# Causal attention of sixteen narrow heads: bf16 parts in one stacked contraction, or fp32 in four strips of the array

## The chip, the cores and the metric

The kernel runs on one core of one Trainium2 chip. The metric is the device time of one execution in microseconds. Before the change the median of three runs is 3485.97 us (3484.61 to 3486.74). A difference of about 0.2% can be told from no change.

## The reference, cut to what matters

The whole kernel is a stack of eight layers on x of 4 batches x 1024 tokens x 128 features, in fp32. The change touches the fifth one alone, causal attention with 16 heads of 8 features each:

```python
def _L1_attn_a_ref(x, WQ, WK, WV, WO):
    mask = jnp.where(jnp.triu(jnp.ones((S, S), dtype=bool), k=1), -jnp.inf, 0.0)
    Q, K, V = (heads(WQ), heads(WK), heads(WV))        # 16 heads of 8 features
    score = jnp.einsum('bhqd,bhkd->bhqk', Q, K) / jnp.sqrt(8)
    score = score + mask
    score = score - jnp.max(score, axis=-1, keepdims=True)
    score = jnp.exp(score)
    score = score / jnp.sum(score, axis=-1, keepdims=True)
    out = jnp.einsum('bhqk,bhkd->bhqd', score, V)
    return out.transpose(0, 2, 1, 3).reshape(B, S, E) @ WO

x = x + _L1_attn_a_ref(_layernorm(x), WQ, WK, WV, WO)
```

## The kernel before, in words

`causal_attention` (line 1010) normalises x, transposes it into FT (L169), projects it (L1277 for Q and K, L1282 for V), and then works in 16 rounds. A round is one batch and one group of four heads. In each round the scores are computed twice. The first pass (L1305) has queries on the partitions and gives only the maximum of each query's row: VectorE reduces each unit out of PSUM (L1450). The maxima are turned (L1313), negated (L1456) and put as extra rows under the queries. The second pass (L1328) has keys on the partitions; its contraction contains that extra row, so the maximum is already subtracted, and ScalarE takes the exponential into the tile PT (L1417). The value product (L1341) then multiplies 128 keys at a time, with four heads side by side in column groups of 32, accumulating in banks 6 and 7. Column 8 of each head's values is all ones, which gives the row's sum.

**bf16 parts.** Q and K are cut into three bf16 parts (L1399, L1432, L1393, L1227), written to DRAM (L1163) and loaded back by `load_round` (L1083, 18 transfers a round) as 9 x 8 = 72 rows, so that one bf16 matmul with 128 rows gives the products of all parts. The maxima, too, are cut into three parts on GpSimd (L1235 to L1242) and sit in three rows from row 96, which L1261 clears. The causal mask is added to a diagonal block by an identity matmul of 128 columns in bf16 (L1308, L1330).

**Units and rings.** The first pass has 38 units a round, each up to one PSUM bank of 512 columns (30 of 512 and 8 of 384); the second pass likewise. First-pass units go through the ring of banks 0 to 2: a unit may start when VectorE has reduced the unit three before it (`s1_free`). Second-pass units go through banks 3 to 5 with ScalarE (`probs`). TensorE's queue is one order written at build time: `items` gives each second-pass unit and each value product a cost, and the first-pass steps of the following rounds are spread between them in proportion. Round r holds the second pass of round r and the first pass of round r+1 from its 19th unit on, and the first 18 units (`LEAD`) of round r+2. A round has 12 value pieces (`items`), with other work between any two of them, so TensorE goes over to the values and back twelve times.

**The sums.** `invert` on SyncE's queue takes the row of sums to 128 partitions, VectorE inverts it (L1464), it goes to DRAM and back broadcast over 8 rows a head (L1193). `divide` multiplies on VectorE (L1468), and two steps a round (`out`, L1318) project the four heads with WO and add to x (L1460).

Of the kernel before, what the change touches and what calls it, by code (L numbers as in the profile page):

```python
# [7 lines left out]
F32 = mybir.dt.float32  # L8
# [6 lines left out]
P = 128  # L15
# [5 lines left out]
BANK = 512  # L21
# [988 lines left out]
def causal_attention(k):  # L1010

    nc, w, bank = k.nc, k.w, k.bank
    HEADS, HD, STRIP = 16, 8, 32
    GROUPS, IN, PARTS = 4, 4, 3
    ROUNDS, SLOTS, RING, SPACES = BATCH * GROUPS, 4, 3, 3  # L1020
    ROWS = PARTS * PARTS * HD
    PEAK = 96
# [3 lines left out]

    QK = k.big[:, 0:SLOTS * GROUP].bitcast(BF16).rearrange("p (s m t) -> p s m t", s=SLOTS, m=2)
    PT = k.big[:, SLOTS * GROUP:(SLOTS + 2) * GROUP].rearrange("p (s h t) -> p s h t", s=2, h=IN)
    FT = k.big[:, SLOTS * GROUP:(SLOTS + 1) * GROUP]
    REST = k.big[:, (SLOTS + 1) * GROUP:(SLOTS + 1) * GROUP + 2 * BANK].rearrange("p (s t) -> p s t", s=2)  # L1030

    parts = [k.big[:, at:at + PARTS * SEQ].bitcast(BF16).rearrange("p (m a t) -> p m a t", m=2, a=PARTS)
             for at in ((SLOTS + 1) * GROUP + 2 * BANK, (SLOTS - 1) * GROUP, (SLOTS - 2) * GROUP)]
# [3 lines left out]
    OT, INV, ON = (z.rearrange("p j d -> p (j d)") for z in zt[1:])  # L1037

    cleared = k.count("causal_cleared")

    def clear(sp, s):

        return sp.dma_start(QK[ROWS:P, s, :, :], k.dram["c_pads"])

    def clear_first(sp):
        for s in range(SLOTS - 2):
            clear(sp, s).then_inc(cleared.sem, 16)

    layernorm(k, turn=(FT, SEQ, 0), sp_first=clear_first)
    inverses = nc.dram_tensor("causal_inverses", (IN, SEQ), F32).ap()  # L1050
    kept = nc.dram_tensor("causal_parts", (2, BATCH, P, PARTS, SEQ), BF16).ap()

    names = ("qk_up", "first", "second", "left", "third", "v_up", "v_in", "fed", "s1_up", "s1_free", "s2_up", "probs",
             "pv", "vs_in", "o_in", "sums_out", "inverse", "sums_in", "peak", "split", "zeroed", "inv_kept", "divided", "ready")
    (qk_up, first, second, left, third, v_up, v_in, fed, s1_up, s1_free, s2_up, probs, pv, vs_in, o_in, sums_out,
     inverse, sums_in, peak, split, zeroed, inv_kept, divided, ready) = [k.count("causal_" + n) for n in names]
    written = [[k.count(f"causal_written{m}{b}") for b in range(BATCH)] for m in range(2)]
    loaded = [k.count(f"causal_loaded{s}") for s in range(SLOTS)]
    peaks_in = [k.count(f"causal_peaks_in{s}") for s in range(SLOTS)]
    with ExitStack() as mem:  # L1060
# [3 lines left out]
        mask = sb("mask", [P, 2, P], BF16)  # L1064
        REST6 = k.arena6[:, TOK:]
        WP = REST6[:, 0:2 * P].rearrange("p (m t) -> p m t", m=2)
        WS = REST6[:, 2 * P:6 * P].rearrange("p (g d) -> p g d", g=GROUPS)
# [3 lines left out]
        low = sb("low", [IN * TPB, 2, P])  # L1071
        lowb = sb("low_parts", [IN * TPB, PARTS, P], BF16)

        def load_round(sp, r, s):

            for m in range(2):
                of_round = kept[m].rearrange("b (g e h) a t -> (b g) e h a t", g=GROUPS, h=IN)
                of_round = of_round[r:r + 1] if isinstance(r, int) else of_round[bass.ds(r, 1)]
                of_round = of_round.rearrange("r e h a t -> (r e) h a t")
                for a in range(PARTS):  # L1080
                    for c in range(PARTS):
                        rows = slice((a * PARTS + c) * HD, (a * PARTS + c + 1) * HD)
                        sp.dma_start(QK[rows, s, m, :].rearrange("e (h t) -> e h t", h=IN), of_round[:, :, a if m else c, :]).then_inc(loaded[s].sem, 16)  # L1083

# [1969 lines left out]
```

## Time and profile before

| what | us |
|---|---|
| median of three runs | 3485.97 |
| the profiled execution, its own time | 3486.21 |
| span of its trace | 3484.3 |
| TensorE matmul busy | 2833.4 (81%) |
| VectorE busy | 2478.2 (71%) |
| ScalarE busy | 1756.8 (50%) |
| GpSimd busy | 1837.0 (53%) |

A busy share of the whole span is an average over eight layers with different limits; the layer that is changed has to be cut out by its window, from about 717 to 1368.7 us. The end of a matmul in the trace is modelled: a 512-column bf16 record is shown some 0.17 us longer than the array streams it, so records that follow each other overlap. In what follows the distance from start to start is used. An fp32 matmul shows as two records.

### The profile page before, as it was taken

The numbers are of one execution on the slowest core, as the hardware profiler recorded it, in microseconds if no ns is written. First come the engines' busy times: TensorE is split into PE (matmuls) and PEld (weight loads), VectorE is DVE, ScalarE is ACT, GpSimd is POOL, SyncE is SP. The second block draws the span as 40 slices with busy tenths as digits, with TensorE's granted clock in tenths as the row PEclk, the third lists the DMA queues.
The fourth block names the chain that finished last, engine by engine and source line by source line (L and its number), as shares of the span: only waits on it lengthen the run. The fifth ranks groups of instructions, "written<-read, shape, count | busy, mean of one in ns | idle before, by whom it ended". The sixth has DMA issues, their size and how long they took to land. (4 is left out here: it accounts for less than half of the span.)

```text
span 3484.3 us, 62796 instructions
## 1 busy us (share of the span) xinstructions
PE 2833.4 (81%) x22143; PEld 1662.3 (48%) x22143; DVE 2478.2 (71%) x4050; ACT 1756.8 (50%) x3569; POOL 1837.0 (53%) x1184
## 2 busy tenths in 40 slices
PE   3677468568999995999999993677677599999998
PEld 1211257443444442677667752223222277757774
DVE  5599646558777763777577755698599777767774
ACT  3544125134556553677467732544444277737762
POOL 3499211130111101888188822698299598729871
PEclk9699678779999997999999996899899899999999
DMA  3355000042222210112112210343054112211121
GB/s 90 79 162 151 8 7 1 8 116 69 38 44 38 44 24 24 38 40 47 30 36 44 43 25 5 109 158 121 31 169 157 56 40 44 45 24 42 42 45 40
DMA packets 176158, 203.21 MB, mean 58 GB/s; under 512 B 108358, under 2 KB 122396, under 8 KB 175388
## 3 DMA queue, kind: packets, MB, share of 16 engines
q1 hardware_dynamic: 175868, 199.41, 22.2%
q8 instruction: 174, 2.85, 0.4%
q14 instruction: 116, 0.95, 0.1%
HBM read 138.36 MB, written 9.44 MB: 42 GB/s over the span
## 5 line engine op out<-in xcount | busy, mean ns | idle before, releaser
L319 POOL TENSOR_TENSOR arena<-arena 128x1024 f32<-128x1024 f32 x192 | 451.3, 2351 | 61.1 <-DVE arena L336 34.0
L1450 DVE TENSOR_REDUCE causal_peak_parts<-psum 128x1 f32<-128x512 f32 (+3 forms) x608 | 375.9, 658 | 114.9 <-PE psum L1308 69.6
L2047 POOL TENSOR_TENSOR arena<-arena,w_minus_half 128x16 f32<-128x16 f32 x128 | 372.5, 2910 | 97.0 <-DVE arena L1954 97.0
L1417 ACT ACTIVATE arena<-psum 128x512 f32<-128x512 f32 (+1 forms) x608 | 304.0, 597 | 229.5 <-PE psum L1330 106.7
L1889 ACT ACTIVATE arena<-psum,arena 128x128 f32<-128x128 f32 x1024 | 277.8, 382 | 252.8 <-DVE arena L1963 252.8
L336 DVE TENSOR_TENSOR_SCAN arena<-psum,arena 128x1024 f32<-128x1024 f32 x160 | 364.6, 2280 | 27.9 <-POOL arena L319 27.9
L289 ACT ACTIVATE psum<-arena,w_A 128x1024 f32<-128x1024 f32 x192 | 214.5, 1118 | 248.5 <-DVE arena L336 211.4
L2054 POOL TENSOR_TENSOR arena<-arena 128x1024 f32<-128x1024 f32 x124 | 292.4, 2358 | 12.6 <-DVE arena L1948 12.6
L1734 PE MATMUL psum<-w_layer_wqkv,arena 128*128 128x512 f32 x512 | 262.7, 638 | 5.7 <-DVE arena L1948 3.7
L262 PE MATMUL psum<-arena,m_sel 96*128 96x512 bf16 x384 | 117.4, 388 | 180.6 <-DVE arena L351 153.0
L1959 DVE COPY arena<-psum 128x512 f32<-128x512 f32 x128 | 88.5, 691 | 238.0 <-PE psum L1746 238.0
L2059 POOL TENSOR_TENSOR arena<-arena 128x1024 f32<-128x1024 f32 x124 | 236.0, 1903 | 19.1 <-POOL arena L2050 19.1
L277 PE MATMUL psum<-arena,w_ident 128*128 128x512 f32 x512 | 243.4, 598 | 0.0
L1328 PE MATMUL psum<-arena 128*128 128x512 bf16 (+3 forms) x768 | 218.6, 331 | 23.5 <-ACT arena L1417 17.1
L1305 PE MATMUL psum<-arena 128*128 128x512 bf16 (+3 forms) x768 | 214.6, 330 | 21.1 <-DMA arena<-causal_parts 11.6
L262 PEld LDWEIGHTS psum<-arena,m_sel 96*128 (+1 forms) x384 | 23.5, 97 | 342.4 <-issue 174.5
L1954 DVE TENSOR_REDUCE arena<-arena 128x16 f32<-128x1024 f32 x128 | 155.1, 1212 | 31.2 <-ACT arena L1867 31.2
L2187 PE MATMUL psum<-arena,w_layer_w 128*128 128x512 f32 (+1 forms) x384 | 176.4, 595 | 0.0
L1341 PE MATMUL psum<-arena,Z 128*32 128x512 f32 (+3 forms) x1536 | 164.9, 503 | 0.3 <-ACT arena L1417 0.3
L179 POOL TENSOR_TENSOR ln_rstd<-ln_var,w_minus_half 128x8 f32<-128x8 f32 x32 | 53.1, 1659 | 208.9 <-DVE ln_var L108 208.9
L1963 DVE TENSOR_REDUCE arena<-psum 128x8 f32<-128x1024 f32 x128 | 156.6, 1224 | 9.2 <-PE psum L1771 9.0
L1328 PEld LDWEIGHTS psum<-arena 128*128 128x128 bf16 x768 | 72.2, 97 | 180.8 <-issue 81.3
(331 smaller groups left out, 6620.7 us busy)
## 6 DMA issues: line engine op xcount, KB each, us to landing
arena<-scan_rows_large SPq DMA_DIRECT2D x128, 512.0 KB, 3.7
arena<-arena SPq DMA_DIRECT2D x256, 130.0 KB, 2.6
arena<-scan_rows_small SPq DMA_DIRECT2D x128, 256.0 KB, 3.8
arena<-causal_parts SPq DMA_DIRECT2D x288, 64.0 KB
causal_parts<-arena SPq DMA_DIRECT2D x8, 768.0 KB, 9.0
arena<-Z SPq DMA_DIRECT2D x128, 32.0 KB, 1.9
arena<-Z SPq DMA_DIRECT2D x32, 128.0 KB
arena<-in_c_pads SPq DMA_DIRECT2D x4, 896.0 KB
```

Of the source, the lines that this page charges most:

```text
L277: mm = pe.matmul(bank[6 + c][0:M, :], fold, weight[:, s % 2, c * BANK:(c + 1) * BANK], start=False, stop=isinstance(j, int) and j == J - 1 ...
L319: pool.tensor_tensor(inputs[:, s % 2], b_lane[:, s % U], du(*runs[o]), ALU.mult).then_inc(input_up.sem, 1)
L336: dve.tensor_tensor_scan(state[s % U], decay(s), inputs[:, s % 2], 0.0, ALU.mult, ALU.add).then_inc(scanned.sem, 1)
L1305: mm = pe.matmul(o, QK[:, s, 0, col + qt * P:col + (qt + 1) * P], QK[:, s, 1, col + half * BANK:col + half * BANK + size], start=True, sto ...
L1328: mm = pe.matmul(o, QK[:, s, 1, col + kt * P:col + (kt + 1) * P], QK[:, s, 0, col + lo:col + hi], start=True, stop=True)
L1417: act.activation(PT[:, kt % 2, heads[0]:heads[0] + len(heads), lo:hi], place, ACT.Exp, scale=SCALE).then_inc(probs.sem, 1)
L1450: dve.tensor_reduce(part[:, heads[0]:heads[0] + len(heads), qt, half:half + 1].rearrange("p h a -> p (h a)"), place[:, 0:len(heads) * size ...
L1734: mm = pe.matmul(bank[pair_of(i) + m], HT[:, s4, :], w["wqkv"][:, m * INNER:(m + 1) * INNER], start=True, stop=True)
L1889: e = act.activation(PR[:, s, h, :], two(3)[:, h * P:(h + 1) * P], ACT.Exp, bias=LOW[:, s, h:h + 1])
L2047: pool.tensor_tensor(RN[:, s4, :], SS[:, s4, :], k.minus_half[:, 0:2 * HEADS], ALU.pow).then_inc(rn_in.sem, 1)
L2054: pool.tensor_tensor(COS[s4], COS[s4], SIN[s4], ALU.add).then_inc(ready2.sem, 1)
L2059: pool.tensor_tensor(heads, heads, RN[:, s4, :].unsqueeze(2).broadcast_to([P, 2 * HEADS, HD]), ALU.mult).then_inc(rot.sem, 1)
```

## The change

Nothing outside `causal_attention` and its constants changes.

- **Scores in fp32.** The parts, their DRAM tensor and the extra casts are gone. Q and K of all heads lie in QD as they come from the projection (ScalarE copies, `qk_in`). `load_round` issues 8 transfers, SBUF to SBUF, that put head i of a group at partitions 32i to 32i+7; row 32i+8 holds the maxima (queries) and ones (keys). A score matmul contracts 8 rows (first pass) or 9 (second pass) of one head's strip of 32 partitions.
- **One head per bank.** A unit is one head's tiles in one bank, 40 units a pass: in the first pass 28 of 512 columns, 8 of 384 and 4 of 256, heads in the order 0, 1, 2, 3; in the second 24 of 512 and 16 of 384, heads 2, 3, 0, 1.
- **Masks.** In the first pass a unit with diagonal blocks (24 of the 40) gets four bf16 matmuls of 32 rows, PICK x MASK, of together 320 columns per diagonal block. In the second pass there is none: GpSimd sets the probabilities of later keys to zero with `affine_select` in PT, 24 instructions a round (`cap_probs`), and the value product waits for them (`capped`).
- **Values.** The same matmuls, in seven visits a round instead of twelve (`follow`), both halves together.
- **Maxima.** No parts: one fp32 row per head is written by four transfers. `split_maxima` and the clearing of rows are gone from GpSimd.
- **Divide** moves from VectorE to GpSimd, between its selects, and waits for `packed`.
- **Output per batch.** `pack` (SyncE's queue) copies each group's 4 x 8 rows into OP; the projection with WO runs twice a batch instead of twice a round.
- **Beginning.** Four of the sixteen Q/K projections and all V projections come first, then scoring starts; the other twelve projections stand between the first pass's units of round 0, one after each second unit. `LEAD` is 20.

```diff
-                        sp.dma_start(QK[rows, s, m, :].rearrange("e (h t) -> e h t", h=IN), of_round[:, :, a if m else c, :]).then_inc(loaded[s].sem, 16)
+                heads = QD[STRIP * g:STRIP * (g + 1), m, b * SEQ:(b + 1) * SEQ]
+                for i in range(IN):
+                    sp.dma_start(QK[STRIP * i:STRIP * i + HD, s, m, :], heads[HD * i:HD * (i + 1)]).then_inc(loaded[s].sem, 16)
...
+        first_groups = [([(0, 0, [0]), (4, 1, [4])], (0, 2)), ([(1, 0, [0, 1]), (5, 1, [5, 4])], (1, 2)),
+                        ([(2, 0, [0, 1, 2])], (2, 1)), ([(3, 0, [0, 1, 2, 3])], (3, 1)),
+                        ([(4, 0, [0, 1, 2, 3])], None), ([(5, 0, [0, 1, 2, 3])], None), ([(6, 0, [0, 1, 2, 3])], None),
+                        ([(6, 1, [4, 5, 6])], (2, 1)), ([(7, 0, [0, 1, 2, 3])], None), ([(7, 1, [4, 5, 6, 7])], (3, 1))]
+        first_units = [(hh,) + u for u in first_groups for hh in range(IN)]
...
+        second_units = [(hh,) + u for u in second_groups for hh in (2, 3, 0, 1)]
...
+        follow = {10: [0], 18: [1], 26: [2], 30: [3], 35: [4], 39: [5], 3: [6, 7]}
...
+                def cap_probs(r, i):
+                    hh, tiles, slot, at, diag, done = second_units[i]
+                    pool.wait_ge(probs.sem, probs.at(r * N2 + i + 1))
+                    place = PT[:, slot, hh, at:at + diag * P].rearrange("p (d t) -> p d t", t=P)
+                    pattern = [[0, diag], [1, P]] if diag > 1 else [[1, P]]
+                    pool.affine_select(place, place, pattern, ALU.is_ge, 0.0, base=0, channel_multiplier=-1).then_inc(capped.sem, 1)
...
+                for r in range(ROUNDS):
+                    for n, i in enumerate(diagonal):
+                        if n == IN:
+                            values(r)
+                        if n == 4 * IN and r:
+                            divide(r - 1)
+                        cap_probs(r, i)
+                divide(ROUNDS - 1)
...
+                        for qt, half, keys in tiles:
+                            runs = [keys] if keys == sorted(keys) else [[x] for x in keys]
+                            for run in runs:
+                                size = len(run) * P
+                                mm = pe.matmul(out[:, at:at + size], QK[rows, s, 0, qt * P:(qt + 1) * P], QK[rows, s, 1, run[0] * P:run[0] * P + size],
+                                               start=at == 0, stop=True, skip_group_check=True)
...
+                            for c in range(4):
+                                mm = pe.matmul(place[:, :, STRIP * c:P], PICK[strip, c, :], MASK[strip, c, 0:diag[1], STRIP * c:P],
+                                               start=False, stop=True, skip_group_check=True)
...
+                for n, step in enumerate(scoring + [("turn", 0)]):
+                    ring_step(step, n, -1)
+                    if n % 2 and ahead < len(CH):
+                        project(ahead)
+                        ahead += 1
```

## Rows read from the trace of the kernel before

**Rows 1.** Busy time by window: us, then PE, PEld, DVE, ACT, POOL, clock, DMA.
```profile
717.00:734.00 17.00, 7.84 (x32) 6.09 (x32) 14.98 (x88) 9.44 (x22) 6.57 (x5) 0.54 0.50 108
734.00:769.50 35.50, 22.81 (x96) 14.39 (x96) 15.75 (x24) 17.93 (x32) 21.56 (x23) 0.82 0.43 115
769.50:805.50 36.00, 26.65 (x140) 10.39 (x140) 33.49 (x60) 1.28 (x1) 1.79 (x5) 0.94 0.62 191
1010.59:1045.28 34.69, 33.31 (x275) 15.12 (x274) 26.55 (x45) 19.81 (x40) 5.29 (x6) 1.00 0.23 43
1322.00:1352.00 30.00, 25.74 (x196) 9.59 (x194) 2.96 (x4) 20.50 (x40) 0.40 (x1) 0.92 0.03 6
```

**Rows 2.** ScalarE's copies of the output, one a round, rounds 1 to 15.
```profile
L1408 ACT COPY Z<-psum x15: 1007/1047/1047, 839.1 to 1324.1; 128x1024 f32<-128x1024 f32 x15
```

**Rows 3.** Timeline of TensorE: scores, then one value product of four heads, scores.
```profile
1000.92 0.22 PE L1308 MATMUL psum<-causal_mask,w_identb 128*128 128x128 bf16 x1
1001.07 1.06 PE L1341 MATMUL psum<-arena,Z 128*32 128x512 f32 x8
1002.07 0.39 PE L1328 MATMUL psum<-arena 128*128 128x512 bf16 x1
1002.29 0.22 PE L1330 MATMUL psum<-causal_mask,w_identb 128*128 128x128 bf16 x1
```

**Rows 4.** Timeline of ScalarE just behind: start, duration, releaser.
```profile
1002.55 0.60 ACT L1417 ACTIVATE arena<-psum 128x512 f32<-128x512 f32 x1 [2.73 <-PE psum L1330]
```

**Rows 5.** Timeline of TensorE: projections, a 2-matmul group and a 4-matmul group in turn.
```profile
739.64 1.88 PE L1277 MATMUL psum<-arena 128*128 128x512 f32 x4
741.36 1.05 PE L1282 MATMUL psum<-w_WV,arena 128*128 128x128 f32 x8
742.25 1.88 PE L1277 MATMUL psum<-arena 128*128 128x512 f32 x4
```

**Rows 6.** Another layer's fp32 scores in four 64x64 tiles: ns min/median/max, first and last start.
```profile
L1771 PE MATMUL psum<-arena x32: 268/269/270, 1500.7 to 1501.5; 64*64 64x128 f32 x32
```

**Rows 7.** Timelines of VectorE and ScalarE where several follow without a wait.
```profile
789.46 3.07 DVE L1450 TENSOR_REDUCE causal_peak_parts<-psum 128x1 f32<-128x512 f32 x5
1324.96 3.28 ACT L1417 ACTIVATE arena<-psum 128x512 f32<-128x512 f32 x7
```

**Rows 8.** Groups by line and form, 734 to 1368 us, VectorE: busy, mean ns, idle.
```profile
L1450 DVE TENSOR_REDUCE causal_peak_parts<-psum 128x1 f32<-128x512 f32 x384 | 249.1, 686 | 65.7 <-PE psum L1305 39.5 <-PE psum L1308 23.1
L1468 DVE TENSOR_TENSOR Z<-Z 128x1024 f32<-128x1024 f32 x16 | 19.5, 1219 | 9.9 <-DMA Z<-causal_inverses 9.9
```

**Rows 9.** The same for GpSimd; the last row is of a later layer (page).
```profile
L1261 POOL MEMSET arena<- 3x4096 bf16 x12 | 42.1, 3506 | 1.7
L1249 POOL COPY Z<-arena 128x256 f32<-128x256 f32 x16 | 6.3, 397 | 218.7 <-PE psum L1341 218.6 <-issue 0.2
L1216 POOL COPY arena<-w_WK 128x128 f32<-128x128 f32 x1 | 0.4, 402 | 0.0
L1227 POOL TENSOR_TENSOR arena<-arena 128x512 bf16<-128x512 f32 x16 | 18.4, 1158 | 6.2 <-ACT arena L1393 6.1
L2054 POOL TENSOR_TENSOR arena<-arena 128x1024 f32<-128x1024 f32 x124 | 292.4, 2358 | 12.6 <-DVE arena L1948 12.6
```

**Rows 10.** The beginning: SyncE's queue and the first score.
```profile
735.16 1.36 SPq L1155 DMA_DIRECT2D arena<-in_L_attn_a_WO  x4
751.17 13.07 SPq L1083 DMA_DIRECT2D arena<-causal_parts  x18
769.65 0.27 PE L1305 MATMUL psum<-arena 128*128 128x128 bf16 x1 [11.58 <-DMA arena<-causal_parts]
```

**Rows 11.** The end of the layer, in order of time.
```profile
1350.83 1.01 ACT L1408 COPY Z<-psum 128x1024 f32<-128x1024 f32 x1 [0.55 <-PE psum L1341]
1357.29 1.28 SPq L1193 DMA_DIRECT2D Z<-causal_inverses  x4
1360.76 1.23 DVE L1468 TENSOR_TENSOR Z<-Z 128x1024 f32<-128x1024 f32 x1 [4.94 <-DMA Z<-causal_inverses]
1362.04 3.78 PE L1318 MATMUL psum<-arena,Z 128*128 128x128 f32 x16 [11.28 <-DVE Z L1468]
```

More of the change, by code:

```diff
@@ L1300, in ring_step @@
                         out = enter(n)
-                        for at, hh in enumerate(heads):
-                            col = hh * SEQ
-                            o = out[:, at * size:(at + 1) * size]
-                            diag = half == (qt * P) // BANK
-                            mm = pe.matmul(o, QK[:, s, 0, col + qt * P:col + (qt + 1) * P], QK[:, s, 1, col + half * BANK:col + half * BANK + size],
-                                           start=True, stop=True)
-                            if diag:
-                                mm = pe.matmul(o[:, size - P:size], k.identb, mask[:, 0, :], start=False, stop=True, skip_group_check=True)
+                        at = 0
@@ L1362, in body @@
-                def body(r, s, before, more, b, g):
-                    steps = ring_steps(before, more)
-                    start = ring_start(r) if before else SHORT + LEAD
-                    fill = b + 1 + (1 if s == 0 and before else 0)
-                    pe.wait_ge(peaks_in[s].sem, peaks_in[s].at(fill * 16 * PARTS))
+                    for half in range(kt // 4, 2):
+                        lo = max(kt * P, half * BANK) - half * BANK
+                        for hh in range(IN):
+                            mm = pe.matmul(bank[6 + half][STRIP * hh:STRIP * (hh + 1), lo:BANK], VS[:, kt, hh, :], probs_place(kt, half, hh),
+                                           start=kt == 0, stop=kt == 4 * half + 3)
@@ L1367, in body @@
+                feed(1)
+                for n, step in enumerate(soon):
+                    ring_step(step, SHORT + n, -1)
+                pe.wait_ge(qk_in.sem, qk_in.at(len(CH)))
+                pe.wait_ge(v_in.sem, v_in.at(TOK // BANK))
+                for r in range(ROUNDS):
+                    steps, start = steps_of(r), ring_start(r)
+                    pe.wait_ge(peaks_in[r % SLOTS].sem, peaks_in[r % SLOTS].at(16 * IN * (r // SLOTS + 1)))
                     done, spent = 0, 0
-                    for kind, at, half, cost in items:
+                    for kind, at, cost in items:
@@ L1402, in _ @@
-                part_two(len(CH) - 1)
+                    act.copy(QD[:, m, c * BANK:(c + 1) * BANK], bank[i if i < 4 else 3 + i % 3]).then_inc(qk_in.sem, 1)
                 def outputs(r):
                     act.wait_ge(pv.sem, pv.at(TPB * (r + 1)))
-                    if not isinstance(r, int) or r:
+                    if r:
                         act.wait_ge(divided.sem, divided.at(r))
                     act.copy(OT, k.psum[:, 6 * BANK:8 * BANK]).then_inc(o_in.sem, 1)
-                def body(r, s, before, more, b, g):
-                    for i, (kt, heads, lo, hi) in enumerate(second_units):
-                        n, size = r * N2 + i, hi - lo
+                for r in range(ROUNDS):
+                    for i, (hh, tiles, slot, at, diag, done) in enumerate(second_units):
+                        n, size = r * N2 + i, sum(hi - lo for _, lo, hi in tiles)
```

458 lines of the change are left out of this document (188 added, 270 removed).

## The prediction, made before the changed kernel was run

> **What bounds the layer now.** I read the windows first: a full round [rows 1] has TensorE busy 33.3 of 34.7 us at full clock (the fourth row), VectorE 26.6, ScalarE 19.8, GpSimd 5.3. The copies of the output confirm the round: 14 steps in 485.0 us, 34.6 each [rows 2]. Busy TensorE is modelled, so I count columns. In bf16, 18432 columns of scores and 4096 of masks in each pass, at 2.4 columns per ns, are 18.8 us a round. An fp32 column costs 1.70 ns: two matmuls of 512 and four of 128 repeat after 2.61 us [rows 5]. The value products are 4608 columns with four heads side by side: the eight records of four heads take 1.00 us until the next score, of which 0.87 is the time of one head alone [rows 3, 5]. So the values are 7.8 us a round. Output and turn add about 2. That is 28.6. The changes to the value product and back cost 0.09 + 0.13 = 0.22 us [rows 3]: 12 visits and the turn, 2.9. The rest of the 34.6, some 3 us, is waiting. TensorE's one ordered queue is the bound; VectorE with 26.6 is second.
>
> **Scores.** Removed: 18.8 us of bf16 columns. Added: 80 units of one head, fp32, 36864 columns, 62.7 us if one runs at a time. The other layer's tiles say they need not: 32 fp32 records of 128 columns start within 0.8 us, 0.026 each, where alone they stand 0.11 apart [rows 5, 6]. That is four at once, on two row halves and two column halves. Four row strips have no row here. I take four at once, nearest to rows 3 and 6: 15.7 us of array time. Then TensorE no longer bounds by columns, and what counts is how long a unit holds its bank. A 512-column unit streams 0.87, then 0.17 until its data is there and 0.04 for the semaphore [rows 3, 4]: 1.08 us, where bf16 needed 0.43. VectorE takes a unit every 0.60 us and ScalarE every 0.45 [rows 7]. With three banks the first-pass ring turns in 1.08 + 0.69 + 0.06 = 1.83, 0.61 a unit; the second-pass ring in 1.74, 0.58. Both just reach the consumers' pace, and every stop is paid in full.
>
> The Trainium skill, TensorE: Matmul & The Clock Gate, section "Part 3: Packing small matmuls", says that matmuls start and end strictly in program order, and gives 3.07x for four row tiles. By the first, each head's two records would hold the next head, and the eight of rows 3 would need five times 0.43; the trace has 1.00 us. By the second, the array time would be 20.4 instead of 15.7 us, which changes nothing as long as the rings bound.
>
> **The visits to the values.** The values use column groups, the scores row strips, so the array must empty at each change. A visit holds back both rings. From the end of one visit to the next start, with n first-pass units between: 0.13 until the first starts, 1.08 until it is taken, (n - 3) x 0.60 until the bank of the last is free, 0.87 + 0.09 to empty, so 2.17 + 0.60(n - 3). By the order of `items`, n is 4, 8, 7, 7, 5, 5, 4: 15.2 + 11.4 = 26.6 us. With values 7.8, the turn 0.9 (its own change, and the maximum of the last unit first), and the masks of the last unit before five visits 1.0 (320 or 640 bf16 columns, 0.13 to 0.27), that is 36.3 us. Seven visits for twelve save 1.1 us of changes, which is already in it. VectorE's own work falls: 28 x 0.60 + 8 x 0.46 + 4 x 0.33 and 0.8 small ones, 22.6, and the divide's 1.22 goes [rows 8]; it does not help, because VectorE now idles during each visit, having at most three units, 1.8 us, in hand.
>
> What stands in the way within a stretch: the queue is one order. A second-pass unit that waits for ScalarE's bank also holds the first-pass unit behind it, and two units of the same head in a row share a strip, 0.87 us. Stepping through the orders by hand, the stretches before the visits to key tiles 0, 1 and 2 have such places: the second pass's head 0 stands directly ahead of the first pass's head 0 (then the masks of four units in a row). I get 1.0 to 1.9 us in each of the three, 4.1 together, less 0.8 for units of 384 columns: 3.3. Bounds: 0 and 5. The round is 39.6 us, own bounds 36.3 and 41.5.
>
> **Beside the path.** GpSimd loses the clearing (3.5 us) and gets the divide, 2.36 us as for that size [rows 9], and 24 selects. No select is in the trace. A copy of 128x128 takes 0.40, a two-input operation of four times that size 1.16, a memset of 4096 elements 3.5 [rows 9]. I take 0.5, nearest to the copy, 12 us a round; bounds 0.4 and 3.5. The visits come one or two groups after the selects they need, so up to about 1.4 us each they are hidden. Loading: 8 transfers instead of 18 a round, issued far ahead; nothing. The output projection, 1.8 us a round with 1.4 on VectorE, stood in every round before and is in the 34.6; now it falls in three of the rounds and is not in the 39.6: 2.0 each with its change of tiling, +6.
>
> **Beginning.** First score: before at 769.65, held by the parts' way through DRAM (11.6 us of idle time) [rows 10]. After: four projections and eight V groups from 734.5, 4 x 0.87 + 8 x 0.89 and some 2 more at the low clock of the start [rows 1], 12.6, and on SyncE 19 transfers at 0.34 [rows 10], eight more and a landing of about 2: 748. The first pass of round 0 then pays for projections: two units, 0.96 and 0.2 of mask, and one projection, 0.87 + 0.22, are 2.2 us, twelve times with a short start 24; 16 units at 0.65, 10.4; the turn 3.7; 20 units at 0.63, 12.6. Together 51, to 799, where the second pass began at 805.5 [rows 1]. Minus 6.5.
>
> **End.** The last round has only the second pass: 7 x 2.17 + 19 x 0.58 + 7.8 = 34.0, say 34.5 with waits, against 30.0 [rows 1]: +4.5. Round 14, with half its first pass: +2. Behind it, divide on GpSimd 2.36 for 1.23 and four packing transfers with their landing, 1.28 + 2.1 by the broadcast's [rows 11]: +4.5.
>
> **Sum.** 14 rounds x (39.6 - 34.6) = 70; + 6 + 2 + 4.5 + 4.5 - 6.5 = +80.5 on the profiled execution's 3486.2: 3566.7, and the median of the runs is 0.2 lower: 3566 us. Beside the rounds that is +10.5. The forecast's own range is 3520 (no blocking, 36.3 a round) to 3593 (41.5).
>
> **Rivals.**
>
> *The visits are cheap (faster).* Place: the two ends of each visit. I charge 1.08 + 0.96 there. If strips finish one after another, so that the last records before a visit are short ones and heads that are ready early feed VectorE sooner (a 384-column unit is ready after 0.86), and units of different strips truly never wait for each other, each of the seven visits and the turn costs 0.5 less and the 3.3 of blocking goes: 32.3 a round. Then 14 x (-2.3) + 10.5 = -22: 3464. For it: VectorE's 22.6 and ScalarE's 17.5 leave the room, and the array has 15.7 us of score columns where it had 18.8. Against: rows 3 and 4, which give the 1.08. The kernel comes out ahead from a round below 33.8, clearly so from 33.4.
>
> *Each head's two records run in program order.* Then every unit adds half its time alone, 31.4 us for both passes; with values 7.8, masks 4.3 and eight visits at 1.2 the round is 53: 14 x 18.4 + 10.5 = +268, 3754. Rows 3 and 6 speak against, since there heads issued one after the other overlap wholly; but there a strip had one matmul waiting, not two. This is the skill's rule above.
>
> *GpSimd's selects.* At 2.0 us each, 48 + 2.8 a round bound everything: 50.8, 14 x 16.2 + 10.5 = +237, 3723. It decides from about 1.4 us a select; the memset's 3.5 for 4096 elements on three partitions speaks against.
>
> *It does not do what it says* in one respect: strips do not overlap at all. 62.7 + 7.8 + 4.3 and visits, 78 a round, 14 x 43.4 + 10.5, about 4104. Rows 6 speak against it; I count it with the second.
>
> **Chances.** Forecast 0.62, cheap visits 0.20, program order (with none overlapping) 0.12, selects 0.06. Below 3479 (0.2%, what can be told from no change) lies the second case but for its edge, and a little of the forecast's lower side: faster 0.20, within 0.2% 0.06, slower 0.74. The range from 3455 to 3670 takes in nearly all of the first two, and leaves most of the last two out.
>
> **What would show it.** In the changed trace: about 39.6 us between ScalarE's copies; the first-pass records of four heads starting within 0.03 us of each other after a visit, and a second one 0.43 later; VectorE's waits for the score line, near 6 a round before, grown to some 15; TensorE's weight loads waiting for ScalarE and VectorE rather than the reverse; GpSimd's selects near 0.5 us and never the releaser of the value product; first score near 748. Wrong would be: a clock below full in a round (fewer strips at work), heads that start 0.4 us apart, or VectorE nearly without a gap.

## The result, and the profile after

The changed kernel takes 4369.09 us (median of 4 runs, 4364.51 to 4376.72), the kernel before 3486.35 (4 runs, 3484.61 to 3486.98): ratio 1.2535, with its 95% interval 1.2513 to 1.2557. Forecast were 3566 us and at most 3670. The sign was right, the size was missed by 803 us, and the time lies beyond every rival too, even the one in which no strips overlap (4104).

Busy time by window of the changed kernel, columns as in [rows 1]: from the projections to the first score, the first pass of round 0, one steady round, the last round.

```profile
734.00:748.00 14.00, 11.37 (x77) 9.21 (x76) 5.53 (x8) 2.34 (x4) 1.54 (x4) 1.00 0.28 62
748.00:880.00 132.00, 130.22 (x440) 61.87 (x437) 44.83 (x75) 14.97 (x26) 2.39 (x8) 0.51 0.04 6
1031.80:1120.40 88.60, 88.60 (x395) 42.55 (x395) 25.82 (x43) 21.82 (x41) 10.49 (x26) 0.52 0.04 7
2170.80:2217.30 46.50, 43.17 (x160) 14.97 (x162) 0.35 (x1) 19.13 (x37) 8.04 (x19) 0.54 0.02 4
```

A steady round takes 88.6 us (three of them, with the output projection, 92.6 to 93.0) where [rows 1] show 34.69. VectorE and ScalarE do nearly what they did before (25.8 and 21.8 us busy), so both stand idle most of the round. The clock column says 1.00 until the first score and then 0.51 to 0.54: the fp32 scores of 8 rows begin at 747.45, from 751 on TensorE runs at 1.2 GHz, and it goes back to 2.4 GHz only for one short stretch in most rounds. In the round shown that stretch is 1053.1 to 1056.5. It stands right behind the longest visit to the values, whose 16 records have 128 rows, and only scores of 8 and 9 rows run in it:

```profile
1049.40 3.64 PE L1305 MATMUL psum<-arena,Z 128*32 128x512 f32 x16
```

In the kernel before, every steady round had 1.00.

ScalarE's copies of the output, one a round, answer to [rows 2]:

```profile
L1364 ACT COPY Z<-psum x16: 1007/1007/1033, 951.8 to 2225.0; 128x1024 f32<-128x1024 f32 x16
```

With the copy before the last at 2178.5 the difference of the two profiled executions, 878.5 us of span (4362.8 less 3484.3), splits up: the first copy comes 112.7 later (951.8 for 839.1), the 14 rounds behind it take 1226.7 for 485.0, which is 741.7, the last round 46.5 for 26.8, which is 19.8, and what follows 4.3. The program of the layers behind is unchanged.

Groups of the layer by line and form: busy, mean ns of one, idle time before and its releaser.

```profile
L1262 PE MATMUL psum<-arena 8*128 8x512 f32 x768 | 568.0, 1062 | 0.8 <-DVE causal_peak_parts L1399 0.8
L1290 PE MATMUL psum<-arena 9*128 9x512 f32 x768 | 479.0, 1039 | 2.5 <-ACT arena L1372 2.4
L1305 PE MATMUL psum<-arena,Z 128*32 128x512 f32 x768 | 180.4, 1051 | 0.0
L1399 DVE TENSOR_REDUCE causal_peak_parts<-psum 128x1 f32<-128x512 f32 x384 | 258.9, 687 | 543.6 <-PE psum L1262 305.0 <-PE psum L1269 225.6 <-remote 12.8
L1372 ACT ACTIVATE arena<-psum 128x512 f32<-128x512 f32 x384 | 218.8, 597 | 574.8 <-PE psum L1290 573.4 <-remote 1.2
L1210 POOL TENSOR_SCALAR_AFFINE_SELECT arena<-arena 128x128 f32<-128x128 f32 x256 | 74.0, 292 | 973.7 <-ACT arena L1372 971.5
```

The consumers are as fast as before (687 ns here, 686 in [rows 8]). What they wait for is PE. A select of 128x128 costs 0.29 us, and the profile never names one as releaser of the value product; at the very last visit, though, the product starts 0.11 us after a select ends and 0.59 after ScalarE does, so there it most likely waited for the select. And VectorE's releaser in a large part of its idle time is L1269, the masks. The timeline of TensorE at a place with diagonal blocks shows why:

```profile
902.54 1.06 PE L1262 MATMUL psum<-arena 8*128 8x128 f32 x4
903.39 0.42 PE L1269 MATMUL psum<-arena 32*128 32x256 bf16 x1
903.40 0.79 PE L1262 MATMUL psum<-arena 8*128 8x256 f32 x1
903.60 0.52 PE L1269 MATMUL psum<-arena 32*128 32x192 bf16 x3
903.98 1.48 PE L1262 MATMUL psum<-arena 8*128 8x256 f32 x5
905.26 0.42 PE L1269 MATMUL psum<-arena 32*128 32x256 bf16 x1
905.27 0.79 PE L1262 MATMUL psum<-arena 8*128 8x256 f32 x1
```

Heads follow each other every 1.87 us (903.40, 905.27), and a head's scores start only as the last head's masks do: the first mask at 903.39 has the next head at 903.40 behind it, 905.26 has 905.27. The forecast had the heads start together.

### The profile page after: what moved, and what is told of

The parts are those of the page before. It is cut to its first block and busy times, and to the rows that moved or that the text cites. A ratio compares the mean times of both kernels' runs of the same rounds, so it can differ in the third digit from the quotient of the medians.

```text
span 4362.8 us, 67024 instructions
## 1 busy us (share of the span) xinstructions
PE 3741.8 (86%) x24123; PEld 2111.9 (48%) x24127; DVE 2461.5 (56%) x4026; ACT 1779.3 (41%) x3585; POOL 1914.5 (44%) x1489
## 3 DMA queue, kind: packets, MB, share of 16 engines
q1 hardware_dynamic: 164724, 177.12, 15.7%
## 5 line engine op out<-in xcount | busy, mean ns | idle before, releaser
L1262 PE MATMUL psum<-arena 8*128 8x512 f32 (+3 forms) x1664 | 940.6, 813 | 3.4 <-DMA arena<-arena 2.6
L1399 DVE TENSOR_REDUCE causal_peak_parts<-psum 128x1 f32<-128x512 f32 (+3 forms) x640 | 401.6, 636 | 955.9 <-PE psum L1269 636.6
L1372 ACT ACTIVATE arena<-psum 128x512 f32<-128x512 f32 (+1 forms) x640 | 334.7, 554 | 1067.1 <-PE psum L1290 1065.4
L1290 PE MATMUL psum<-arena 9*128 9x512 f32 (+3 forms) x1536 | 715.9, 838 | 5.1 <-ACT arena L1372 4.9
L1210 POOL TENSOR_SCALAR_AFFINE_SELECT arena<-arena 128x128 f32<-128x128 f32 (+1 forms) x384 | 125.2, 330 | 1309.8 <-ACT arena L1372 1307.3
L1262 PEld LDWEIGHTS psum<-arena 8*128 8x128 f32 x1664 | 385.3, 303 | 93.4 <-issue 60.7
L1290 PEld LDWEIGHTS psum<-arena 9*128 9x128 f32 x1536 | 290.6, 297 | 284.0 <-issue 210.5
L1269 PEld LDWEIGHTS psum<-arena 32*128 32x128 bf16 x1536 | 195.1, 144 | 258.8 <-issue 244.2
L1305 PE MATMUL psum<-arena,Z 128*32 128x512 f32 (+3 forms) x1536 | 269.5, 843 | 0.0
L1269 PE MATMUL psum<-arena 32*128 32x64 bf16 (+5 forms) x1536 | 211.6, 284 | 0.0
```

The source lines that it names most:

```text
L1262: mm = pe.matmul(out[:, at:at + size], QK[rows, s, 0, qt * P:(qt + 1) * P], QK[rows, s, 1, run[0] * P:run[0] * P + size], start=at == 0, s ...
L1269: mm = pe.matmul(place[:, :, STRIP * c:P], PICK[strip, c, :], MASK[strip, c, 0:diag[1], STRIP * c:P], start=False, stop=True, skip_group_c ...
L1290: mm = pe.matmul(bank[RING + n % RING][:, at:at + hi - lo], QK[rows, s, 1, kt * P:(kt + 1) * P], QK[rows, s, 0, lo:hi], start=at == 0, sto ...
L1305: mm = pe.matmul(bank[6 + half][STRIP * hh:STRIP * (hh + 1), lo:BANK], VS[:, kt, hh, :], probs_place(kt, half, hh), start=kt == 0, stop=kt ...
L1372: act.activation(PT[:, slot, hh, at:at + size], bank[RING + n % RING][:, 0:size], ACT.Exp, scale=SCALE).then_inc(probs.sem, 1)
L1399: dve.tensor_reduce(spot, place[:, 0:len(tiles) * size].rearrange("p (h t) -> p h t", t=size), AX_X, ALU.max).then_inc(s1_free.sem, 1)
```

## The experiments

**The strips by themselves.** A kernel of its own with twelve streams of 512-column matmuls. Its core:

```diff
+            for i in range(192):
+                m = f32(strip(i % 4, 8), bank[i % 4], i // 4 % 4)
...
+            for i in range(96):
+                f32(strip(i % 4, 8), bank[i % 4], i // 4 % 4)
+                for c in range(4):
+                    m = b16(strip(i % 4, 32), bank[i % 4], P - 32 * c, False, c)
```

> The eight layers are left out; x is returned as it came. TensorE runs twelve stretches of matmuls of 512 columns, each after an idle time of some 12 us: fp32 with 128 rows; fp32 with 8 rows in one strip; the same over four strips in turn; fp32 with 32 rows in one strip; the same over four strips; bf16 with 8, 72 and 128 rows; fp32 8 rows over four strips, each followed by four bf16 mask matmuls in its own strip; the same matmuls with the masks of four strips interleaved; the first mask pattern with 32 rows; fp32 with 64 rows over two halves. Theory of the clock (few rows at work): the granted clock stays 0.5 in the stretches with 8 rows in one strip (0.87 us becomes 1.7 a matmul), and is 1.0 with 128 rows; four strips of 32 rows reach 1.0. Rival (the clock fell for another reason, such as changes of tiling): 1.0 after the first few us in every stretch. Theory of the strips: four strips in turn need a quarter of one strip's time per matmul at equal clock; rival (program order holds both records): half of it. Theory of the masks: with the four masks behind each score in its strip the heads no longer overlap and a unit costs about 0.87 + 0.2 us at full clock; interleaved masks bring it under half of that.

Windows inside the twelve streams, in order (columns: us, matmuls, weight loads, VectorE, GpSimd, clock, DMA): fp32 of 128 rows; 8 rows in one strip; 8 rows, four strips in turn; 32 rows, one strip; 32 rows, four strips; bf16 of 8, 72 and 128 rows; fp32 of 8 rows with four masks behind each score; the same work with the masks of four strips interleaved; 32 rows with masks behind each score; fp32 of 64 rows over two halves in turn.

```profile
76.00:98.00 22.00, 22.00 (x53) 9.69 (x51) 0.00 (x0) 0.00 (x0) 1.00 0.00 1
112.00:192.00 80.00, 80.00 (x95) 31.00 (x95) 0.00 (x0) 0.00 (x0) 0.50 0.00 0
207.00:288.00 81.00, 81.00 (x380) 33.44 (x384) 0.00 (x0) 0.00 (x0) 0.50 0.00 1
303.00:383.00 80.00, 80.00 (x95) 30.74 (x94) 0.00 (x0) 0.00 (x0) 0.50 0.00 0
418.00:439.00 21.00, 21.00 (x204) 9.53 (x200) 0.00 (x0) 0.00 (x0) 1.00 0.00 1
455.00:521.00 66.00, 66.00 (x156) 22.63 (x155) 0.00 (x0) 0.00 (x0) 0.50 0.00 0
536.00:602.00 66.00, 66.00 (x156) 22.79 (x155) 0.00 (x0) 0.00 (x0) 0.50 0.00 0
635.00:653.00 18.00, 18.00 (x85) 8.20 (x84) 0.00 (x0) 0.00 (x0) 1.00 0.01 1
668.00:846.00 178.00, 178.00 (x572) 61.21 (x571) 0.00 (x0) 0.00 (x0) 0.50 0.00 0
861.00:911.00 50.00, 50.00 (x560) 22.38 (x556) 0.00 (x0) 0.00 (x0) 0.50 0.01 2
926.00:1104.00 178.00, 178.00 (x571) 61.18 (x570) 0.00 (x0) 0.00 (x0) 0.50 0.00 0
1140.00:1162.00 22.00, 22.00 (x106) 9.76 (x104) 0.00 (x0) 0.00 (x0) 1.00 0.00 1
```

Read the first number in brackets (matmul records) against the length, and the clock. Three things follow.

- *Strips do overlap.* The third row has 380 records in 81 us, some 213 ns each, the second 95 in 80, some 842. Four strips are four times as fast as one, with two records of a head waiting in each. The array time of 15.7 us was right: at full clock (fifth row) it is 21 / 204 = 103 ns a record, and the 36864 score columns of a round, worth 144 records of 512, come to 14.8 us.
- *The clock.* All these windows have TensorE busy without a gap. Four strips of 8 rows are at 0.50, four strips of 32 rows at 1.00, one strip of 32 rows at 0.50, bf16 of 8 and of 72 rows at 0.50, of 128 rows at 1.00, two halves of 64 rows at 1.00. The rival of the expectation, 1.0 after the first few us in every stretch, is refuted.
- *The masks.* With four of them behind each score the heads do not overlap at all: 96 units in 180.1 us, 1.88 each, the 1.87 of the kernel's timeline. The same matmuls with the strips alternating take 51.8 us, 0.54 a unit, both at 0.50. And 32 rows do not bring the clock up as long as the masks keep the strips apart (last row but one).

The Trainium skill, TensorE: Matmul & The Clock Gate, section "Part 1: The HAM clock gate", ties the clock to how busy the engine has been. Taken as the busy time of the profile, the trace does not agree: the steady round above is busy for 88.60 of 88.60 us at 0.52.

**The masks out.** The first-pass masks are left out of the changed kernel; the maximum then also runs over later keys of the diagonal blocks.

```diff
-                        if diag:
+                        if False:
```

> The kernel after, without the four mask matmuls of the first pass. The row maximum is then taken over some later keys too, which changes no probability. Theory of the masks (24 of 40 units fill their strip's queue and hold the next head): the round falls from 88.6 us by far more than the masks' own 8.5 us at half clock, to about 60, still at clock 0.5. Rival (heads do not overlap at all, masks only add their columns): 88.6 - 8.5 = 80.

Measured: 4065.43 us (one run), 68.2 a round; theory had about 60, the rival 80, so the truth lies between, and the masks cost well over their own 8.5 us. A window of one round, and TensorE's timeline behind a visit:

```profile
1047.50:1115.80 68.30, 68.30 (x300) 31.18 (x298) 25.26 (x43) 21.64 (x43) 10.46 (x26) 0.55 0.05 9
```
```profile
1111.46 1.22 PE L1290 MATMUL psum<-arena 9*128 9x512 f32 x1
1111.47 1.22 PE L1262 MATMUL psum<-arena 8*128 8x512 f32 x1
1111.48 1.22 PE L1290 MATMUL psum<-arena 9*128 9x512 f32 x1
1111.48 1.22 PE L1262 MATMUL psum<-arena 8*128 8x512 f32 x1
1112.48 1.06 PE L1290 MATMUL psum<-arena 9*128 9x512 f32 x1
```

The masks cost 20.4 us a round (88.6 less 68.2) at half clock. Now four heads start within 0.02 us, as forecast, but their second records come 1.02 later, not 0.43, since the clock stays low.

**32 rows a strip.** The changed kernel, masks and all, with the scores contracted over all 32 rows of a strip (Q and K zeroed once at the start, so that 23 of the 32 rows are zero):

```diff
+                pool.memset(QK, 0.0).then_inc(emptied.sem, 1)
...
-                        rows = slice(STRIP * hh, STRIP * hh + HD)
+                        rows = slice(STRIP * hh, STRIP * (hh + 1))
...
-                    rows = slice(STRIP * hh, STRIP * hh + HD + 1)
+                    rows = slice(STRIP * hh, STRIP * (hh + 1))
```

> The kernel after with all 32 rows of a strip contracted in both passes, the rows 9 to 31 zero; the order and number of matmuls and their columns are the same. The first pass then adds an older maximum to its scores, so the probabilities are not those of the reference; one memset of 8192 columns is added at the beginning. Theory of the clock (8 rows of a strip are too little work for the clock to be granted): the clock in the rounds rises from 0.52 to near 1.0 and the round from 88.6 to about 46 us. Rival (clock lost by gaps or changes of tiling, or the zeros count as idle): clock 0.5 and 88.6 us as before.

Measured: 4000.57 us (one run), 58.0 a round at clock 0.85; theory had about 46 near 1.0, the rival 88.6 at 0.5.

```profile
1101.60:1159.60 58.00, 58.00 (x396) 28.84 (x394) 25.84 (x43) 21.39 (x42) 10.46 (x26) 0.85 0.06 11
```

The same matmuls with the same columns in every round, rows added of which all but one a strip are zero, and the round is 30.6 us shorter. Only the rows at work differ, and with them the clock. That it stops at 0.85 and not 1.00 fits the stream of 32 rows with masks behind each score, which stood at 0.50. The added memset (6.9 us, before the first loads) is a cost of the experiment itself: the first score comes at 763.48 here and at 755.42 in the next run, for 747.45.

**Both.** 32 rows and no first-pass masks, the two edits above together.

> Both edits at once: all 32 rows of each strip contracted (rows 9 to 31 zero) and no mask matmuls in the first pass. Theory (two causes that multiply: half clock, and masks that keep the heads from overlapping): the clock stays at 1.0 and the round is what was forecast for free strips without masks, 39.6 less 1.0 for masks and part of the blocking: 36 to 39 us, the time about 3505 to 3550. The two causes together must then explain 88.6 - 38 = 50 us a round. Rival (something third, such as the changes to the value product or the waits for the selects, holds the round): over 45 us a round, 3650 or more.

```profile
760.00:820.00 60.00, 58.20 (x111) 21.32 (x112) 23.20 (x39) 7.73 (x12) 0.00 (x0) 0.50 0.06 9
891.70:933.73 42.03, 41.63 (x300) 20.26 (x298) 25.04 (x43) 21.19 (x42) 10.48 (x26) 1.00 0.09 15
```

Measured: 3703.86 us (3697.75 to 3705.61, 4 runs), ratio to the kernel before 1.0608 (1.0585 to 1.0631). Most of what was lost is back. A round at full clock takes 42.03 us, above the theory's 36 to 39 and below the rival's 45; the whole time lies where the rival had it, for another reason. Against the kernel before the profiled run is 216.5 us longer: 52.6 up to the first copy of the output, 137.7 in 14 rounds, 19.4 in the last, 6.9 behind it. The beginning still runs at 0.50 (first row) and so does the last round (0.55); why strips of 32 rows do not bring the clock up there, no run separates. Eight of the thirteen steady rounds have a spell of low clock (0.87 to 0.96) and take 43.7 to 51.9 us. Three of these also hold the output projection; the one at 0.96 takes 47.6 where rounds without it take 43.7 at the same clock, so the projection costs 3.9 and not the 2.0 forecast. And the rounds at full clock take 42.03 us where the forecast, without its 1.0 for masks, gives 38.6. The timeline behind a visit at full clock shows four strips starting together again, and their second records 0.54 later; the records behind those follow after 0.43 (932.10):

```profile
931.13 0.69 PE L1293 MATMUL psum<-arena 32*128 32x512 f32 x1
931.14 0.69 PE L1265 MATMUL psum<-arena 32*128 32x512 f32 x1
931.15 0.69 PE L1293 MATMUL psum<-arena 32*128 32x512 f32 x1
931.15 0.69 PE L1265 MATMUL psum<-arena 32*128 32x512 f32 x1
931.67 0.59 PE L1293 MATMUL psum<-arena 32*128 32x512 f32 x1
```

**Masks of two heads interleaved,** 32 rows (and `OUT_AT` 31 for 30, to keep the pairs together):

```diff
+                            held.append((hh, out))
+                            if hh % 2 == 0:
+                                return
...
+                                for h, o in held:
+                                    strip = slice(STRIP * h, STRIP * (h + 1))
+                                    mm = pe.matmul(place[:, :, STRIP * c:P], PICK[strip, c, :], ...)
```

> 32 rows, and the first pass's masks kept but issued for two heads together: head 0's scores, head 1's scores, then the eight masks of the two heads in turn; the same for heads 2 and 3. Matmuls, columns and bytes as in the run with 32 rows, whose round is 58.0 us. Theory of the masks (four masks right behind a head's scores fill its strip's queue, so that the next head starts late): two heads overlap, and the round falls to 44 to 50 us with the clock near 1.0. Rival (the masks cost by themselves, wherever they stand): 58 stays, within 2 us.

Measured: 3880.55 us (one run), rounds of 50.6 to 62.7, the shortest at clock 0.93:

```profile
1030.10:1080.70 50.60, 50.57 (x396) 25.29 (x394) 24.69 (x43) 21.39 (x42) 10.42 (x26) 0.93 0.07 12
```

With the same matmuls in another order, this round is 7.4 us shorter than 58.0; over the thirteen steady rounds the mean falls from 62.0 to 56.8. Part of what the masks cost is their order. The clock rose as well (0.80 to 0.84 over these rounds), and most of the gain is that: by length times clock, an estimate, 49.3 us at full clock became 47.1 in the rounds of 58.0 and 50.6. The range expected was just missed by the shortest round and by more in all others, and five of the thirteen lie within 2 us of the rival's 58.

**The kernel before without its first-pass masks:**

```diff
-                            if diag:
-                                mm = pe.matmul(o[:, size - P:size], k.identb, mask[:, 0, :], start=False, stop=True, skip_group_check=True)
```

> The kernel before, without the 32 identity matmuls a round that mask the first pass (4096 bf16 columns, 1.7 us). The maximum over some later keys is subtracted instead, which changes no probability. TensorE's queue bounds the round there: 34.6 us falls by 1.2 to 1.7, the time by 19 to 27 us, to about 3463. Rival (rings and VectorE bound the round): under 0.5 a round, 3478 to 3486.

```profile
1002.40:1036.20 33.80, 32.05 (x244) 12.85 (x242) 26.50 (x45) 19.58 (x41) 5.34 (x7) 1.00 0.19 43
```

Measured: 3471.87 us (6 runs) against 3488.14, ratio 0.9959 (0.9946 to 0.9972); a round of 33.75, so 0.93 us less, somewhat under what was expected. The expectation was missed, and its rival (under 0.5 a round) too. Masks by matmul, 4096 columns a round or 1.7 us, cost 0.93 us where they run behind full-width scores; 10240 columns, 8.5 us at half clock, cost 20.4 where they stand between strips.

**Selects for masks in the kernel before:** no first-pass masks, and GpSimd's selects in place of those of the second pass, 22 a round.

```diff
+                    def cap(n):
+                        pool.wait_ge(probs.sem, probs.at(r * N2 + n + 1))
...
+                            pool.affine_select(place, place, [[0, len(heads)], [1, P]], ALU.is_ge, 0.0, base=0, channel_multiplier=-1).then_inc(capped.sem, 1)
...
-                        if lo == kt * P:
-                            mm = pe.matmul(o[:, 0:P], k.identb, mask[:, 1, :], start=False, stop=True, skip_group_check=True)
...
+                    pe.wait_ge(capped.sem, capped.at(r * NC + caps[kt]))
```

> The kernel before without the first pass's masks (as in the run of that name, 33.75 us a round) and also without the second pass's identity masks (32 x 128 bf16 columns, 1.7 us a round); GpSimd zeroes the probabilities of later keys instead, 22 selects a round at 0.3 to 0.5 us. Queue theory: the round falls by the 0.9 that the first 1.7 us gave, to about 32.8, the time to about 3457. Rival (GpSimd's selects, with its 3.5 us memset between, come late for the value product): 34 or more, 3475 or slower.

```profile
998.90:1031.30 32.40, 30.00 (x208) 10.90 (x210) 26.32 (x45) 19.68 (x41) 12.79 (x29) 1.00 0.25 41
```

Measured: 3458.73 us (3448.34 to 3460.53, 4 runs) against 3491.28, ratio 0.9901 (0.9876 to 0.9926), 32.36 a round. It is 1% faster than the kernel before: this part of the change was worth having, on the bf16 scores.

**72 rows in the kernel before.** If few rows lower the clock, the kernel before should lose it when its zero rows are left out (72 rows in the first pass, 99 in the second; the edit of the second is not shown):

```diff
-                            mm = pe.matmul(o, QK[:, s, 0, ...], QK[:, s, 1, ...],
+                            mm = pe.matmul(o, QK[0:ROWS, s, 0, ...], QK[0:ROWS, s, 1, ...],
...
```

> The kernel before, with the first pass contracting only its 72 rows of parts instead of all 128 (rows 72 to 127 hold zeros and ones that give nothing), and the second pass 99 rows instead of 128. The same number of matmuls and columns. Theory of the clock (rows at work decide): the granted clock in the rounds falls from 1.00 and the round rises, to over 50 us if it stays at 0.5. Rival (only strips lose the clock; zero rows do nothing): 34.7 us and clock 1.00 as before.

```profile
1021.80:1056.60 34.80, 33.51 (x275) 15.32 (x274) 26.50 (x45) 19.83 (x40) 5.25 (x7) 1.00 0.19 41
```

Measured: 3497.86 us (one run), 34.85 a round, clock 1.00. A miss, although the stream of 72 rows alone stood at 0.50. That stream had begun after idle time, this work had not. The next run takes that up.

**After warm work.** The streams again; six begin with 160 bf16 records of 128 rows and go on without a gap.

```diff
+            warm()
+            for i in range(160):
+                m = b16(slice(0, 72), bank[i % 4], c=i % 4)
```

> A kernel of its own, leaving out all layers: only streams of 512-column matmuls on TensorE, in eight stretches with idle time of TensorE between them. Open is why the round of the kernel before kept full clock with scores of 72 and 99 rows, while bf16 matmuls of 72 rows that started after idle time stayed at 0.50. Six stretches begin with 160 bf16 records of 128 rows and go on without a gap: (1) 160 bf16 of 72 rows, (2) 160 bf16 of 8 rows, (3) 192 fp32 of 8 rows, four strips in turn, (4) 192 fp32 of 32 rows, four strips in turn, (7) 48 fp32 of 32 rows in one strip, (8) 192 fp32 of 16 rows, four strips in turn. (5) has four bf16 of 72 rows and then one of 128, again and again, from idle; (6) bf16 of 99 rows from idle. Theory A, the clock once full is held by work that could not have brought it up: 72 rows keep 1.00 in (1), some 35 us of 216 ns each; (2), (3) and (7) still fall to 0.50, as the steady rounds of the changed kernel did. Theory B, it goes by the rows at work alone, and it was the value products and masks of 128 and 64 rows that held it in the kernel before: (1) falls to 0.50 (about 68 us), and (5) with one record of five at 128 rows comes to 1.00. Under both (4) stays at 1.00. (6) and (8) place the border between the cases: A and B both leave them open, I expect (6) at 1.00 and (8) at 0.50.

Windows in the second part of the streams (1), (2), (3) and (4), in the mixed stream (5), in (6), and in the second part of (7) and (8):

```profile
100.00:125.00 25.00, 25.00 (x117) 11.37 (x116) 0.00 (x0) 0.00 (x0) 1.00 0.00 1
190.00:238.00 48.00, 48.00 (x114) 16.46 (x112) 0.00 (x0) 0.00 (x0) 0.50 0.00 0
300.00:360.00 60.00, 60.00 (x286) 25.79 (x284) 0.00 (x0) 0.00 (x0) 0.50 0.00 1
420.00:455.00 35.00, 35.00 (x332) 16.76 (x328) 0.00 (x0) 0.00 (x0) 1.00 0.00 1
480.00:550.00 70.00, 69.33 (x163) 24.12 (x165) 0.00 (x0) 0.00 (x0) 0.50 0.00 0
575.00:602.00 27.00, 27.00 (x127) 12.23 (x126) 0.00 (x0) 0.00 (x0) 1.00 0.00 1
665.00:725.00 60.00, 60.00 (x72) 23.05 (x71) 0.00 (x0) 0.00 (x0) 0.50 0.00 0
785.00:820.00 35.00, 35.00 (x332) 16.76 (x328) 0.00 (x0) 0.00 (x0) 1.00 0.00 1
```

Theory A holds, and B falls on both counts. 72 rows behind warm work stay at 1.00 (first row), and the mixture that contains a record of 128 rows in every five, begun after idle time, stays at 0.50 (fifth). A full clock is kept by work that did not raise it from idle. Not by any work, though: 8 rows, four strips of 8, one strip of 32 are at 0.50 after the same warm start. Four strips of 16 rows kept 1.00, against what I expected of (8). (Strips of 16 rows were not tried from idle.) So the kernel before holds its clock with 72 rows, and the changed kernel, with 32 to 36 rows at work at best and 8 where masks keep the strips apart, loses it, gets it back in most rounds behind the longest visit to the values, and loses it again.

**Where the other 3.4 us are.** Two kernels on the base of "both" (32 rows, no first-pass masks). In the first the value products of key tiles 1 to 5 are left out, in the second those of key tiles 1 to 7 are cut to 128 columns.

```diff
+                    if 0 < kt < 6:
+                        pe.matmul(bank[6 + kt // 4][:, BANK - 1:BANK], PICK[0:STRIP, 0, :], MASK[0:STRIP, 0, 0, 0:1], ...).then_inc(pv.sem, 1)
+                        return
```

> The changed kernel with strips of 32 rows and no first-pass masks (42.03 us a round at full clock, forecast 38.6), and besides that the value products of key tiles 1 to 5 are left out: of seven visits a round two stay (key tile 0, and 6 with 7); in place of each of the five stands one matmul of a single column in the tiling of the scores, behind the same waits. Open: where the 3.4 us are that the round takes above the forecast. By the terms of the prediction a visit costs 2.17 + 0.60 (n - 3) where the ring alone would take 0.61 n, so 0.37 more, and the values left out are 3200 of 4608 columns, 5.4 us: 5 x 0.37 + 5.4 = 7.3 us less. If the rings are what was mis-sized, the gain is about that: 34.7 us a round, with the 3.4 us still in it. If the emptying and refilling of the array at a visit was mis-sized (3.4 / 7, 0.5 us each), it is 2.4 us more: 32.3. I look at rounds at full clock.

> The same base (32 rows, no first-pass masks, 42.03 us a round), with all seven visits, but each value product of key tiles 1 to 7 has 128 columns at most, so half of the 4608 columns are left out. Their array time was put at 7.8 us a round, wholly on the path: 3.9 us less, 38.1. If VectorE's or ScalarE's pace bounds instead and the visits are partly hidden behind it, the round shrinks by less than 2 us (above 40.0).

Their rounds at full clock, one window each:

```profile
1184.70:1220.50 35.80, 35.19 (x243) 20.19 (x242) 25.05 (x44) 21.44 (x42) 10.36 (x26) 1.00 0.10 17
```
```profile
970.00:1008.20 38.20, 37.80 (x300) 20.45 (x298) 25.06 (x43) 21.18 (x42) 10.32 (x26) 1.00 0.09 16
```

Measured: 3650.82 and 3687.43 us (one run each). Half the value columns are worth 3.8 us, as forecast (3.9), so the array time of the values was right and on the path. Five visits less are worth 6.2 us, not 7.3 and far from 9.7: the visits cost no more than they were charged, rather less. That figure rests on the one steady round of this kernel that kept full clock. By elimination the 3.4 us lie in the units between the visits, that is in the two rings and in the order of the queue, or in the turn; no run shows it directly. Both kernels also lost the clock more often than their base: over the thirteen steady rounds it was 0.85 and 0.86, where the base had 0.95. With less value work between the scores, low rounds took up to 56 us.

## Why the prediction was wrong

**The step that failed first is one that had no term:** the clock, taken as full throughout. The forecast took every duration of the rounds from rows at 1.00 [rows 1, 3, 5] and carried it over to scores of 8 and 9 rows. It named the case itself under what would be wrong, "a clock below full in a round (fewer strips at work)", and gave it neither a price nor a chance. The price: with the masks in, 32 rows bring the round from 88.6 to 58.0, 30.6 us; without them from 68.2 to 42.0, 26.2. Over the whole program the rows of zeros took off 369 us with masks (4369.09 to 4000.57) and 362 without (4065.43 to 3703.86), though they do not bring the full clock back in the beginning and the end.

**Masks between strips: 1.0 forecast, 16.0 to 20.4 measured.** These figures are not at full clock: 20.4 is at half, and in 16.0 (58.0 less 42.0) the clock rose from 0.85 to 1.00 too. By length times clock, an estimate, a round holds 46 to 49 us of full-clock work with the masks and 38 to 42 without, so the masks themselves are 7 to 9 us, half of it their own 4.3 us of columns, which the forecast took to be hidden. Only the masks just ahead of a visit were charged, the others were thought to stream beside other heads. They do not. The timeline and the streams (1.88 us a unit behind one another, 0.54 interleaved) show that several matmuls of one strip in a row hold back the next strip. What the forecast said of rows 3 and 6, that there a strip had one matmul waiting and not two, was the right doubt: the two records of a score did no harm, a score with four masks behind it did. How many it takes was not tried.

**Four strips at once: right** (213 ns against 842, four times and not the 3.07 of the prediction's second price). With that the rival "program order of each head's two records" falls where no masks stand between, and by itself the mechanism is refuted. In the units with masks something close to its second form, no overlap, is what happened.

**Visits and values: right or slightly dear.** Half the value columns were worth 3.8 us for 3.9, five visits 6.2 for 7.3. **The rings are too cheap by 3.4 us a round** at full clock (42.0 for 38.6). That VectorE would idle some 15 us a round was right there (25.0 busy of 42.0). Which of the places it is, the second record that comes 0.54 after the first and not 0.43 behind a visit, or more blocking between the passes than 3.3, was not separated and stays open.

**Cheap visits (the faster case): refuted.** Even with the masks out and at full clock a round takes 42.03 us, where this rival had 32.3 and the kernel before 34.7. **GpSimd's selects: refuted,** 0.29 us for 128x128 and 0.41 for 128x256, under the 0.5 taken.

**Beginning and end.** The first score came at 747.45, forecast 748. But the second pass began at 859.25 and not at 799, since the first pass of round 0 ran at 0.51. The last round is 19.8 us longer (4.5 forecast), at clock 0.54; with 32 rows it is 37.65 us at 0.75. The tail behind the last copy is 4.3 us longer, forecast 4.5. One slip of the working changes nothing: the round's upper bound, 36.3 and 5 of blocking, is 41.3 and not 41.5.

**The sum** that would have met it: 14 rounds at about 53 more each, 742, and 137 beside them, where the forecast had -6.5 + 4.5 + 4.5 = 2.5 (the other 8 of its 10.5 lay in the rounds). That the sign came out right says little for the sum: the mechanism that set the time was not in it.

## What to carry to other kernels

Before splitting a contraction of 128 rows into narrow strips, ask what the clock will do: busy time does not answer it, and here the scores of 8 rows slowed all that shares the queue, the untouched value products too (1051 ns a record of 512 columns, 611 in the kernel before). Alternate the strips; here a score followed by its own corrections in the same strip was serial work. And take a rewrite apart: the selects with the masks gone were worth 1% on the old kernel, while the whole cost 25%.

## What the runs showed of the hardware

- The granted clock follows more than busy time. With TensorE busy without a gap in the profile: fp32 on four strips of 8 rows 0.50, of 16 rows 1.00 (after warm work), of 32 rows 1.00; one strip of 32 rows 0.50; bf16 of 72 rows 0.50 after idle time and 1.00 after warm work; 99 rows 1.00 after idle time.
- Rows of zeros are enough to raise it: contracting 32 rows a strip, 23 of them zero, for 8 or 9 took 30.6 us out of a round.
- fp32 records of four strips overlap fully: 213 ns each at half clock, 103 to 105 at full, against 842 for one strip at half clock.
- One head's fp32 score with four bf16 matmuls behind it in the same strip takes 1.88 us at half clock, and the next strip waits; interleaved over four strips it is 0.54.
